# Output of the first feed-forward: scaled and rounded by ScalarE, its bias added by TensorE, the gated addition one pair later

## What is computed

```python
def _L0_ffn_ref(x, w1, b1, w2, b2):
    h = jnp.einsum('bsd,df->bsf', x, w1) + b1
    h = float2fix(h, MANT_BITS)                    # multiples of 2^-8
    h = pwlin_gelu_basic(h, MANT_BITS, MANT_BITS)  # 33 knots, linear between them
    h = float2fix(h, MANT_BITS)
    out = jnp.einsum('bsf,fd->bsd', h, w2) + b2
    return float2fix(out, MANT_BITS)
...
x = x + jnp.tanh(g_xattn[0]) * _L0_xattn_ref(_layernorm(x), ctx_512, ctx_512, ...)
x = x + jnp.tanh(g_ffn[0]) * _L0_ffn_ref(_layernorm(x), w1, b1, w2, b2)
x = x + jnp.tanh(g_xattn[1]) * _L1_xattn_ref(_layernorm(x), ctx_512, ctx_512, ...)
x = x + jnp.tanh(g_ffn[1]) * _L1_ffn_ref(_layernorm(x), wg, w1, b1, w2, b2)   # 8 experts, top 2
```

## Time and profile before

| | |
|---|---|
| median of 3 runs | 549.48 us (549.39 to 550.75) |
| the profiled execution's own time | 551.23 us |
| its span, first to last instruction | 549.5 us |
| TensorE, matmuls | 497.6 us busy, 91% of the span |
| VectorE | 401.8 us, 73% |
| ScalarE | 259.8 us, 47% |
| GpSimd | 146.6 us, 27% |

### The profile page before, as it was taken

How to read it: one execution, slowest core, us unless ns; L and a number is a source line. 1 busy time by engine, 2 the same in 40 slices (tenths; PEclk the granted TensorE clock), 3 DMA queues, 4 the chain that set the end, 5 groups by cost and what they waited for, 6 DMA issues and landing times.

```text
span 549.5 us, 8680 instructions
## 1 busy us (share of the span) xinstructions
PE 497.6 (91%) x3292; PEld 421.4 (77%) x3292; DVE 401.8 (73%) x747; ACT 259.8 (47%) x418; POOL 146.6 (27%) x120
## 2 busy tenths in 40 slices
PE   5999996989797989999999975999999999999991
PEld 3687766879697868767787732898899999999991
DVE  4277699999999886958977878665776657667441
ACT  1266858576674355435655522435353453444220
POOL 4223410001000111302212201721517346282253
PEclk9999998999998999979999995999999999999996
DMA  7302110000000011211221340304437465462031
GB/s 230 115 2 78 40 37 0 2 0 1 1 1 2 0 39 39 69 47 40 78 78 40 110 159 3 95 20 95 126 114 154 93 177 115 150 147 60 7 39 20
DMA packets 34694, 36.01 MB, mean 66 GB/s; under 512 B 3892, under 2 KB 33501, under 8 KB 34525
## 3 DMA queue, kind: packets, MB, share of 16 engines
q1 hardware_dynamic: 28509, 27.80, 16.0%
q0 software_dynamic: 6144, 7.66, 8.5%
HBM read 27.80 MB, written 8.39 MB: 66 GB/s over the span
## 4 chain that ended last, share of the span: by engine, by line
PE 62%; DVE 24%; issue 7%; ACT 3%; DMA 1%; POOL 0%; SPq 0%; DVEq 0%; POOLq 0%; ACTq 0%
PE PS L1371 13%; PE PS L1372 13%; PE PS L1373 13%; PE PS L1741 5%; PE PS L1389 3%; PE PS L1614 3%; PE PS L1685 3%; DVE tmp L1034 2%; DVE tmp L1045 2%; PE PS L1750 2%; DVE hT_lo L1053 2%; DVE tmp L1025 2%; DVE st L911 2%; DVE tmp L1022 2%; PE PS L1464 1%
## 5 line engine op out<-in xcount | busy, mean ns | idle before, releaser
L1371 PE MATMUL PS<-w_hi,hT_hi 128*128 128x256 f32 x384 | 111.9, 291 | 4.3 <-DVE hT_lo L1053 4.1
L1372 PE MATMUL PS<-w_lo,hT_hi 128*128 128x256 f32 x384 | 110.4, 287 | 0.0
L1373 PE MATMUL PS<-w_hi,hT_lo 128*128 128x256 f32 x384 | 110.2, 287 | 0.0
L883 ACT ACTIVATE tmp<-PS,biasT 128x512 f32<-128x512 f32 (+1 forms) x80 | 43.8, 599 | 111.7 <-PE PS L1373 111.7
L625 POOL DMA_INDIRECT out<-tmp,dst_idx x32 | 55.8, 1743 | 99.8 <-DVE tmp L1327 93.1
L1371 PE MATMUL PS<-xT_hi,w_hi 128*128 128x512 f32 (+1 forms) x224 | 81.1, 362 | 0.4 <-DVE xT_lo L935 0.4
L1372 PE MATMUL PS<-xT_lo,w_hi 128*128 128x512 f32 (+1 forms) x224 | 80.7, 360 | 0.0
L1371 PEld LDWEIGHTS PS<-w_hi,hT_hi 128*128 128x128 f32 x384 | 75.3, 196 | 6.8 <-DVE hT_lo L1053 4.7
L1373 PE MATMUL PS<-xT_hi,w_lo 128*128 128x512 f32 (+1 forms) x224 | 80.4, 359 | 0.0
L1372 PEld LDWEIGHTS PS<-w_lo,hT_hi 128*128 128x128 f32 x384 | 75.5, 197 | 1.0
L1373 PEld LDWEIGHTS PS<-w_hi,hT_lo 128*128 128x128 f32 x384 | 75.4, 196 | 0.0
(11 more groups left out here) (225 smaller groups left out, 907.5 us busy)
## 6 DMA issues: line engine op xcount, KB each, us to landing
w_raw<-in_L_ffn_w SPq DMA_DIRECT2D x72, 256.0 KB, 3.3
residual<-in_x SPq DMA_DIRECT2D x4, 512.0 KB, 4.5
out<-residual SPq DMA_DIRECT2D x3, 512.0 KB, 4.6
normed_rows<-xn SPq DMA_DIRECT2D x3, 512.0 KB, 2.9
kv<-in_L_ffn_b SPq DMA_DIRECT2D x1, 1024.0 KB, 6.4
tmp<-in_L_xattn_Wq SPq DMA_DIRECT2D x2, 256.0 KB, 5.3
out<-residual SPq DMA_DIRECT2D x2, 256.0 KB, 4.1
normed_rows<-xn SPq DMA_DIRECT2D x2, 256.0 KB, 2.2
```

Source lines behind the costliest of these rows:

```text
L883: act.activation(gD[:, G % 2, f, 0:P * n], H[:, G % 2, f, 0:P * n], ACT.Gelu, bias=biasT[:, col:col + 1]).then_inc(e_gelu, 1)
L1371: pe.matmul(o, lh, rh, start=start, stop=False, skip_group_check=skip)
L1372: pe.matmul(o, lh, rl, start=False, stop=False, skip_group_check=skip)
L1373: return pe.matmul(o, ll, rh, start=False, stop=stop, skip_group_check=skip)
```

## The change

ScalarE, not VectorE, reads `O`, multiplies by 256 and writes the integers: an activation (`Copy`, scale 256) of 128 x 1024. The bias no longer comes in there. TensorE puts it into `O` as the first of what is added up there: at the first `project` of each chunk two matmuls of 512 columns, whose weights `ones_b2` have ones in partitions 0 and 32 and zeros between them, and whose moving data `b2_hl` have the bias's high part in partition 0 and its low part in partition 32. VectorE makes both in stage A, in a corner of `w_lo` that is free until stage C. The transfer of the bias goes to 33 partitions rather than 128. `ffn_residual` stays on VectorE, one pair later: behind `segment(7)`, `(11)` and `(15)`.

The pieces below are, in order: the names, the transfer, three pieces of ScalarE (the last in stage C's loop over tiles `t`), `output_units` and four pieces of VectorE, and `project` of TensorE.

```diff
+        b2_hl, ones_b2 = w_lo[0:33, 7, 0, 0, :], w_lo[0:33, 7, 0, 1, 0:P]
+        b2_raw = b2_bc[0:33, :]
...
-                             (b2_bc[:, :], b2_0.partition_broadcast(P)),
+                             (b2_raw, b2_0.partition_broadcast(33)),
...
+            def ffn_output(c):
+                act.wait_ge(hT_used, PAIRS * (c + 1))
+                act.wait_ge(tr_ready, NC + c + 2)
+                act.activation(xn[:, (c + 1) % 2, :, :].bitcast(I32), O, ACT.Copy, scale=256.0).then_inc(o_free, 1)
...
+                if g % PAIRS == 2 and PAIRS < g < NB_PAIRS:
+                    ffn_output(g // PAIRS - 1)
...
+                    if t == 0:
+                        ffn_output(NC - 1)
...
             def output_units():
                 dve.wait_ge(late_loaded, 48)
-                dve.tensor_scalar(b2_bc[:, :], b2_bc[:, :], 256.0, None, ALU.mult).then_inc(late_split, 1)
+                dve.memset(ones_b2.bitcast(F32), 0.0)
+                link(dve.tensor_copy(b2_hl, b2_raw))
+                for row in (0, 32):
+                    dve.tensor_copy(ones_b2[row:row + 1, :], ones_bf[row:row + 1, :])
+                dve.tensor_tensor(b2_hl[32:33, :], b2_raw[32:33], b2_hl[32:33, :].bitcast(F32),
+                                  ALU.subtract).then_inc(late_split, 1)
...
-            def ffn_output(c):
-                dve.wait_ge(hT_used, PAIRS * (c + 1))
-                dve.wait_ge(tr_ready, NC + c + 2)
-                dve.scalar_tensor_tensor(out=xn[:, (c + 1) % 2, :, :].bitcast(I32), in0=O, scalar=256.0, in1=bcast(b2_bc[:, :].unsqueeze(1), [P, 4, D]),
-                                         op0=ALU.mult, op1=ALU.add).then_inc(o_free, 1)
...
                     segment(g)
+                    if g % PAIRS == PAIRS - 1 and g > PAIRS:
+                        ffn_residual(g // PAIRS - 1)
...
-                    if g % PAIRS == 2 and g > PAIRS:
-                        ffn_output(g // PAIRS - 1)
-                        ffn_residual(g // PAIRS - 1)
...
-                if g == NB_PAIRS + LAG - 1:
-                    ffn_output(NC - 1)
...
                     pe.wait_ge(o_free, n)
+                if p == 0 and g < NB_PAIRS:
+                    pe.wait_ge(late_split, 2)
+                    for half in range(2):
+                        pe.matmul(O[:, 2 * half:2 * half + 2, :], ones_b2, bcast(b2_hl.unsqueeze(1), [33, 2, D]),
+                                  start=True, stop=False, skip_group_check=True)
```

More of the change, by code:

```diff
@@ L1581, in project @@
                         w = [a[:, u % RING, 1, f, :] for a in (w_hi, w_lo)]
-                        first = p == 0 and f == 0 and (i % 2 == 0 or alone)
+                        first = p == 0 and f == 0 and (i % 2 == 0 or alone) and g >= NB_PAIRS
                         last = p == PAIRS - 1 and f == 1 and (i % 2 == 1 or alone)
```

## The result

| | before | after |
|---|---|---|
| median, 11 executions each | 550.64 us (547.49 to 555.81) | 546.60 us (544.20 to 549.89) |
| ratio after / before, 95% interval | | 0.9942 (0.9921 to 0.9964) |
| span of the profiled execution | 549.5 us | 542.7 us |

A forecast was written before the change was run, and what follows sets the result against it. VectorE's queue was taken to bound stage B from about 60 to 174.78 us, then TensorE to 187. Gains 0.30 + 1.74 + 0.25 = 2.3 us took the median from 549.48 to 547.2; range 545.2 to 549.7.

The forecast's parts named there:

- the entry: Start of stage B on VectorE: first interpolation 0.3 us earlier, between 1.1 earlier and 0.9 later.
- the seam: From stage B to C: shorter copy on ScalarE and statistics out of VectorE's way gain 0.25 us.
- the three places: Middle of stage B, copy handed to ScalarE and addition one pair later: 0.84, 0.45 and 0.45 us gained.
- The bias matmuls: Eight added on TensorE in stage B, ahead of its holes: cost nothing; without cover up to 3.8 us.
- Stage A: VectorE's bias group held by GpSimd's subtraction: next maximum 2.15 us late, 0.1 to 0.4 remaining at the first segment.
- the term that follows: VectorE's second segment goes before GpSimd's subtraction; the interpolation, let in at 68.65, starts 0.3 us earlier.
- the third rival: More gain: 3.06 us hole filled, low clock gone, pair 0's interpolation not held, 1.1 each: 545.2 us; chance 0.12.
- the wait for `O`: TensorE at the third chunk's end waits perhaps 0.7 us, ahead of its 3.06 us hole.
- The first rival: Stage A's delay not absorbed, low clock before the first hidden: entry costs 1.5 us, 549.0 us; chance 0.15.

The follow-up runs named there:

- run of the group in idle time: Changed kernel with VectorE's five bias instructions moved out of stage A's row, behind x_lo(4) and the shifts; ratio to the kernel before 0.9933.
- run of the group alone: Kernel before plus only VectorE's five bias instructions in stage A, their result unused; ratio to the kernel before 0.9960.
- run with x_lo behind it: Kernel with the addition behind the interpolation, with x_lo of each chunk's second pair moved behind the interpolation too; ratio to the kernel before 0.9840.

## Why the prediction was right, and where not

The direction, the median (546.60 in 545.2 to 549.7) and most terms held. Forecast were 2.3 us; measured were 3.2 by the ratio and 3.45 by the traces. That the sum came as near as it did is partly luck: 0.83 us of the gain come from a low clock that went away, which the forecast of 2.3 did not contain. Of the 1.15 us between 2.3 and 3.45, 0.56 lie at the entry, 0.38 at the seam and 0.11 each at the three places and behind the seam. Point by point:

- **The three places.** Forecast 0.84, 0.45 and 0.45, measured 0.87, 0.52 and 0.46. (The forecast took 4.94 us for both later places; the trace of before has 4.99 at the second, from 137.00 to 141.99, and 4.93 at the third.) The wait for the copy is 0.52 us (forecast 0.6), the copy 1.01 (taken 1.05). The old place for the addition cost 2.04 us of waiting: the prediction's point, that VectorE waits for part of what it no longer does, is the right reading, and the last step (a later place) takes the rest.
- **The bias matmuls** at nothing: right, and shown by the run with four times as many. But the holes named as cover, 2.49 and 3.06 us, were not there any more: 0.85 and 0.27 us were left of them, and the result was the same.
- **Stage A.** The mechanism was right: the group is held by GpSimd's subtraction, the next maximum 1.90 us late (forecast 2.15), the first segment 0.10 late. The first `hidden` was 1.2 late (forecast 1.4). The order at the second segment turned as forecast. What was mis-sized is the term that follows. I put GpSimd's end at 27.45 us after the mark and took 0.3 us of gain; it ended at 27.05, and the interpolation that it held, begun at 64.23, was done 1.1 us after its release, not 1.3. That gives 0.86. The run of the group in idle time and the run of the group alone both show that it hangs on this order.
- **The seam.** Forecast 0.25 us for the shorter copy and the statistics out of VectorE's way; measured 0.63, for another reason. The step that failed is that TensorE's last projects would keep their time, only earlier. TensorE came to the last hole no earlier than before, VectorE 2.7 us earlier, 0.27 us are left of 3.06, and the low clock of the earlier trace rows did not follow. That is worth 0.83 us (7.27 against 6.44 in the run with the last copy on VectorE). It was a part of the third rival, and happened. What holds TensorE back has several parts, which no run separates: the wait for `O`, the bias, and the low clock in the third chunk. The term as forecast had the wrong sign: the copy on ScalarE costs 0.2 there.
- **The first rival** (a low clock behind the new hole before the first `hidden`): the hole came, 1.51 us, and the clock stayed at 1.00 behind it. Two of the other runs showed what the rival describes, at another hole (4.13 and 3.50 us), and it cost them 1.4 us at the third place.
- **The wait for `O`** was expected at the end of the third chunk; it came at the second (1.32 us) and, in the profile after, not at the third. It stands ahead of a hole of 2.10 us, and VectorE waits for TensorE nowhere behind it in stage B.
- **The third rival's sum** is 545.0, not 545.2, if 1.1 us are added at each of its two places.

## What to carry to other kernels

When work is handed to an engine that gets its input later, ask first where in its old engine's queue the consumer stands: with the hand-over alone the three places took 2.2 us more, with the consumer one pair later they took 1.9 less than before, and with it behind one more step stage B gave another 1.8. Before reading two profiles against each other, take a mark behind the first loads and compare distances; 3.35 us of the difference of the spans lay ahead of the mark, and two profiles of one kernel differed by 3.1 there. Then look for stretches of low clock that only one of the two has: one took back 1.4 us at the third place, one is worth 3.0 in stage C, and both came and went without a change that explains them.

## What the runs showed of the hardware

- GpSimd's subtraction does not hold VectorE from its recorded start. A cast of 33 x 256 that starts 0.12 us behind it takes 0.22 us; one of a single row that starts 0.38 behind it takes 2.24, and one of 16 columns 0.20 behind it 2.32. A single-column instruction 0.20 us behind it took 0.15. With two SBUF inputs the interpolation was held as well: 1.75 us instead of 1.22, and 3.42 in the run with x_lo behind it. The Trainium skill (SBUF — State Buffer, section "Who interferes with whom") gives the shared port pair to whichever of VectorE and GpSimd issues first, for its whole instruction. The long rows agree (2.24 and 2.32 us). The one of 0.22 us at 0.12 behind the recorded start doesn't, unless GpSimd's recorded start lies ahead of the moment at which it takes the pair, which no run here shows.
- The length of a hole doesn't fix whether the clock falls: in the first profile of before it stayed full behind 3.35 us (ahead of the transposes of chunk 3), and it fell behind 2.49 and 3.06 us; in the second it fell behind 4.11 us at that same place and stayed full behind 1.92 at the end of B. In the changed kernel it fell behind 2.10 us and stayed full behind 1.51. How long it stays low varies as well: behind 4.11 us the mean of 9 us was 0.81, behind 4.13 us in the run of the group alone 0.62.
- A stretch of low clock in stage C was there in the first profile of before and not in the second; over 14 profiles it goes with 3.0 us.
- Added work made a kernel faster: five instructions in stage A bring 0.7 to 0.9 us at the entry of stage B, because they delay GpSimd's subtraction by 1.0 us and VectorE's segment by only 0.1, so that the segment no longer meets it.
